# A two-layer transformer tower: in its first layer GpSimd divides the third weight and makes the state B's product with v and its count, and that weight's scales are made ahead of the mixes

## The chip, the cores and the metric

The kernel runs on one core of a Trainium2 chip (trn2). The metric is the time of one execution on the device in microseconds (us). It is the median of a few runs; one further execution was taken by the profiler, and all rows of a trace below come from that one. The engines are called PE (TensorE, matrix products), DVE (VectorE), ACT (ScalarE), POOL (GpSimd) and SP (the queue that issues most DMAs). Each runs its own list of instructions in order and waits on semaphores that others raise.

## What is computed

64 images are cut into 16 patches each and embedded in 256 features; with a class token that makes 64 x 17 = 1088 tokens. Layer 0 adds a recurrent attention and a feed-forward part whose weights and tokens are rounded to 4-bit values with a scale for each block of 16; layer 1 adds softmax attention with 16 heads and a mixture of 64 experts. The change is in the attention and in the preparation of the feed-forward weights of layer 0:

```python
# x: the normalised tokens; xx: the same, shifted by one token inside an image
# k, v, r = (x * mu_s + xx * (1 - mu_s)) @ W_s          (three "mixes")
def step(carry, inp):
    A, Bacc = carry
    kt, vt, ct, mt = inp          # ct = max(t - 1, 0), mt = (t > 0)
    out = A + jnp.exp(u + kt) * (vt * Bacc + ct)
    ek = jnp.exp(kt)
    A = e_dec * A + mt * ek * vt
    Bacc = e_grow * Bacc + mt / ek
    return ((A, Bacc), out)
# attention = (sigmoid(r) * out) @ Wo, added to h

def fake_quant_nvfp4(x, global_scale):       # of gate, up and down weights, and of tokens
    amax = max |x| of a block of 16
    sc8 = e4m3(clip(amax / 6 * global_scale, 0, 448)); dq = sc8 / global_scale
    a = clip(|x| / dq, 0, 6)                 # "divides"
    return sign(x) * nearest_fp4(a) * dq
```

global_scale of a weight is 448 * 6 / max|w| over the whole matrix.

## The kernel before, in words

Features lie on the 128 partitions in two halves (o or c = 0, 1), tokens along the free dimension (N = 1088, image by image, T = 17). Tokens by rows are kept in `h` in 9 tiles of 128 (NT). A layer norm is made in two parts, tiles 0 to 5 and 6 to 8 (LN_PARTS): ACT takes squares (L1172), DVE makes the variance `veps` (L1487, `ln_variance`), POOL raises it to -1/2 (L595, `ln` of POOL), DVE finishes it with one step of Newton (L1493 to L1497, `ln_finish`), ACT writes the normalised tile `xn` (L1180), PE transposes it (L726) and ACT moves it to `nT` (L1189).

Then, all in lists written out by hand:

- ACT makes six shifted copies of `nT`, one for each of k, v, r and half (L1234); DVE adds the unshifted part in six mixes (L1616), in the same order; PE multiplies them with the weights in six groups of 4 column quarters (L786, order k0, v0, k1, v1, r0, r1); ACT evacuates them: exp(k) to `ekk` and exp(-k) to `dB` (L1258, L1260), v to `vv` (L1265), sigmoid(r) to `sig` (L1256). `s_rkv_ev` counts the quarters, 4 a group.
- DVE's states, for each half o: the scan of B into `sB` (L1628), the input of A (L1632), B's product with v (L1637), the scan of A into `sA` (L1639), the count added to B's product (L1642), times exp(u) and exp(k) (L1643), the sum (L1646), and the gate with sigmoid(r) (L1623, `gated_state`), written over `vv`, which raises `s_y0`. A `link` waits for the end of an operation before the next.
- PE multiplies the gated halves with the output weight (L805, 8 tiles of half 0 after the first `s_y0`, 8 of half 1 after the second, then both of the last tile), and DVE adds them to `h` (L1468).

The third (down) weight is prepared among this: `weight_maxima(2)` on DVE (L1554, L1561), `largest(2)`, an all-reduce over partitions on POOL (L600), which stands in POOL's list behind both pows of the first norm; `weight_scales(2)` on DVE between the two first operations of the scans (L1565 to L1569, L1502 to L1512, then `weight_divide`, L1537, two operations of 128x1024); ACT's absolute value (L1198, `weight_size(2)`), behind the evacuation of r; DVE's rounding (L1516 and L1520) before and between the additions to `h`. The scales read the all-reduce's result, the division reads the scales.

POOL does the division for the nine tiles of hidden values later in the layer (L623), in the same form as the third weight's.

The last stage of layer 1 waits for nine semaphores `s_back`, one for each tile of rows brought back by DMA, from SP's list.

Of the kernel before, what the change touches and what calls it, by code (L numbers as in the profile page):

```python
# [15 lines left out]
ALU = mybir.AluOpType  # L16
# [9 lines left out]
CH = 4  # L26
# [82 lines left out]
def build(nc, A, out):  # L109
    with ExitStack() as ctx:  # L110
        def sem(name):
            return ctx.enter_context(nc.semaphore(name))

        def sems(name, n):
            return [sem(f"{name}{i}") for i in range(n)]
# [232 lines left out]
        s_scanz = sem("s_scanz")  # L348
        s_scanA = sem("s_scanA")
        s_wdiv = sem("s_wdiv")  # L350
# [86 lines left out]
        s_slot = sem("s_slot")  # L437
        s_back = sems("s_back", NT)
        s_sum = sem("s_sum")
# [127 lines left out]
        def _(pool):  # L567
# [29 lines left out]
            def largest(m):  # L597
# [12 lines left out]
                                    pattern=[[1, P]], channel_multiplier=-1).then_inc(s_mc, 1)  # L610
            ln(0, 0)
            ln(0, 1)
            largest(2)
            ln(1, 0)
# [99 lines left out]
        def _(pe):  # L714
# [426 lines left out]
            def row_sums(t):  # L1141

                pe.wait_ge(s_back[t], 16)
                for k in range(TOPK):
                    mm = nc.tensor.matmul(ps[0:rows(t), SUM_BANK[t], 0:D], ident[0:rows(t), 0:rows(t)],
                                          picked[t][0:rows(t), k * D:(k + 1) * D], start=False, stop=(k == TOPK - 1))
                mm.then_inc(s_sum, 1)
# [306 lines left out]
        def _(dve):  # L1454
# [22 lines left out]
            def after(count):  # L1477
                dve.wait_ge(s_dve, count)
# [52 lines left out]

            def weight_divide(x, scale, m):

                if m == 2:
                    for j in range(2):
                        v = x[:, j * I0:(j + 1) * I0].rearrange("p (k b r) -> p k b r", k=PAIRS, r=2)
                        ins = V.tensor_tensor(v, v, bc(bc(scale[:, j * NHB:(j + 1) * NHB], 1, PAIRS), 3, 2), ALU.mult)  # L1537
                    return ins
                x = x.rearrange("p (b k) -> p b k", k=BLK)
                return V.tensor_tensor(x, x, bc(scale, 2, BLK), ALU.mult)  # L1540
# [22 lines left out]
            def weight_scales(m):  # L1563
                dve.wait_ge(s_wmxa, m + 1)
                link(V.reciprocal(gsc[:, m:m + 1], wmx_all[:, m:m + 1]))  # L1565
                link(V.tensor_scalar(gsc[:, m:m + 1], gsc[:, m:m + 1], 448.0 * 6.0, None, ALU.mult))
                link(V.tensor_scalar(gs6[:, m:m + 1], gsc[:, m:m + 1], 1.0 / 6.0, None, ALU.mult))
                link(V.reciprocal(gin[:, m:m + 1], gsc[:, m:m + 1]))
                link(V.tensor_scalar(gil[:, m:m + 1], gin[:, m:m + 1], -(1.0 - 2.0 ** -23), None, ALU.mult))  # L1569
                link(block_scales(wam[:, m, :], [wsc[:, i, :] for i in range(3)], wscm, wscb[0] if m == 2 else wscb[m][:, 0:NBW], m, m == 2))  # L1570
                weight_divide(wraw[m], wsc[:, 2, :], m).then_inc(s_wdiv, 1)

# [37 lines left out]
            V.memset(dB.rearrange("p c (b t) -> p (c b) t", t=T)[:, :, 0:2], 0.0).then_inc(s_scanz, 1)  # L1610
            ln_finish(0, 1)
            dve.wait_ge(s_mixz, 4)
            for i, s in enumerate((1, 2, 0)):
# [10 lines left out]

            for o in range(DC):
                dve.wait_ge(s_d0, 7)
                dve.wait_ge(s_rkv_ev, (2 * o + 1) * CH)
                done_b = mark(V.tensor_tensor_scan(sB[o], d0[:, 2 * o + 1, :], dB[:, o, :], 0.0, ALU.mult, ALU.add))  # L1628
                if o == 0:
                    weight_scales(2)  # L1630
                dve.wait_ge(s_rkv_ev, (2 * o + 2) * CH)
                done_a = mark(V.tensor_tensor(dA[:, o, :, 2:T], by_t(ekk[:, o, :])[:, :, 1:T - 1],  # L1632
                                              by_t(vv[:, o, :])[:, :, 1:T - 1], ALU.mult))
                if o == 1:
                    gated_state(0)
                after(done_b)
                done_b = mark(V.tensor_tensor(sB[o], sB[o], vv[:, o, :], ALU.mult))  # L1637
                after(done_a)
                done_a = mark(V.tensor_tensor_scan(sA[o], d0[:, 2 * o, :], dA[:, o, :, :].rearrange("p b t -> p (b t)"), 0.0,  # L1639
                                                   ALU.mult, ALU.add))  # L1640
                after(done_b)
                link(V.tensor_tensor(by_t(sB[o]), by_t(sB[o]), bc(cnt, 1, B), ALU.add))  # L1642
                link(V.scalar_tensor_tensor(out=sB[o], in0=sB[o], scalar=eu[:, o:o + 1], in1=ekk[:, o, :],  # L1643
                                            op0=ALU.mult, op1=ALU.mult))
                after(done_a)
                link(V.tensor_tensor(sA[o], sA[o], sB[o], ALU.add))  # L1646
            gated_state(1)

# [310 lines left out]
            def add_rows_of(t):  # L1959

                r = slice(0, rows(t))
                dve.wait_ge(s_back[t], 16)
                p = picked[t][r, :].rearrange("p (k d) -> p k d", k=TOPK)
# [82 lines left out]
```

## Time and profile before

| | us |
|---|---|
| median of 3 runs | 623.29 |
| lowest and highest | 622.12, 624.65 |
| the profiled execution, its own time | 625.0 |
| its span in the trace | 623.3 |
| DVE busy | 439.4 (70%) |
| PE busy | 518.0 (83%) |
| ACT busy | 337.6 (54%) |
| POOL busy | 218.7 (35%) |

The profiled execution took 1.7 us more than both its span and the median. Start times below are in us from the start of the span. In a row of a timeline stand the start, the time in us, the engine, the line, the operation, the tile written and those read, shapes and count; in brackets, how long the engine had been idle before it and what ended that ("issue": nothing that the profile shows). `region` is the name of two large buffers from which most tiles are cut. Spans on POOL are rough.

### The profile page before, as it was taken

The page shows a single profiled execution, that of the slowest core. Times are in us where ns is not written, and L with a number is a line of the kernel's source. Part 1 is how long each engine was busy: PE and PEld are TensorE (multiplying, and loading weights), DVE is VectorE, ACT ScalarE, POOL GpSimd, SP SyncE. Part 2 cuts the span into 40 slices and gives each one's busy share as a digit, 9 for nine tenths or more (in the row PEclk, how much of TensorE's full clock was granted, in tenths as well). Part 3 has the DMA queues.
Part 4 walks back from the last instruction along what each step waited for, and adds up shares of the span by engine and source line. Part 5 has one row for each costly group of instructions (what it writes and reads, how often), then busy time and mean ns, then how long its engine had stood idle before and what let it go on. Part 6 is the DMA issues. An engine that isn't in the chain of part 4 may idle for free.

```text
span 623.3 us, 10367 instructions
## 1 busy us (share of the span) xinstructions
PE 518.0 (83%) x3494; PEld 421.2 (68%) x3498; DVE 439.4 (70%) x995; ACT 337.6 (54%) x798; POOL 218.7 (35%) x230
## 2 busy tenths in 40 slices
PE   3986953166555699999999999999999999999875
PEld 2755842023323699999999887876777777777674
DVE  4996998999999546555655713576776777775676
ACT  1577635255444656666666325625666677676600
POOL 2101001022422602222221141237777777777600
PEclk9985987586875699999999999999999999999979
DMA  8980000008200000000000001013777777887492
GB/s 270 381 315 0 1 0 0 0 2 272 79 2 0 1 26 27 26 28 27 26 1 2 2 1 51 22 28 100 200 225 203 230 237 216 230 241 212 143 407 87
DMA packets 43895, 67.33 MB, mean 108 GB/s; under 512 B 11022, under 2 KB 27015, under 8 KB 43716
## 3 DMA queue, kind: packets, MB, share of 16 engines
q1 hardware_dynamic: 36868, 64.62, 32.5%
q0 software_dynamic: 6976, 2.07, 1.7%
q8 instruction: 28, 0.46, 0.3%
q14 instruction: 23, 0.19, 0.1%
HBM read 66.81 MB, written 17.20 MB: 135 GB/s over the span
## 4 chain that ended last, share of the span: by engine, by line
PE 60%; DVE 24%; DMA 5%; ACT 4%; issue 3%; POOL 3%; SPq 0%; DVEq 0%; POOLq 0%; ACTq 0%
PE ps L1089 9%; PE ps L734 6%; PE ps L736 6%; PE ps L735 6%; PE ps L953 5%; PE ps L911 5%; PE ps L786 4%; PE ps L741 4%; DMA region<-x_rows,region 3%; PE ps L943 3%; PE ps L1079 2%; PE ps L925 2%; PE ps L1136 2%; DVE region L1724 2%; PE ps L1097 2%
## 5 line engine op out<-in xcount | busy, mean ns | idle before, releaser
L1089 PE MATMUL ps<-region 128*128 128x352 f32 x256 | 86.4, 460 | 0.3 <-issue 0.3
L1780 DVE TENSOR_TENSOR region<-ps,region 32x136 f32<-32x136 f32 x128 | 38.1, 298 | 55.3 <-PE ps L911 53.8
L685 POOL DMA_INDIRECT region<-x_rows,region x64 | 68.1, 1064 | 20.2 <-issue 15.0
L734 PE MATMUL ps<-nTh,high 128*128 128x272 f32 (+2 forms) x248 | 74.4, 300 | 0.4 <-ACT region L1362 0.4
L735 PE MATMUL ps<-nTl,high 128*128 128x272 f32 (+2 forms) x248 | 71.6, 289 | 0.0
L694 POOL DMA_INDIRECT y_rows<-region x60 | 61.1, 1019 | 21.0 <-issue 14.7
L644 POOL COPY region<-region 32x544 f32<-32x544 f32 x32 | 26.4, 825 | 115.1 <-DVE region L1799 113.6
L1928 DVE SCALAR_TENSOR_TENSOR region<-region,ps 128x176 f32<-128x176 f32 x64 | 25.4, 397 | 42.9 <-ACT region L1439 40.3
L736 PE MATMUL ps<-nTh,pairs_low 128*128 128x272 f32 x192 | 55.6, 290 | 0.0
L1449 ACT ACTIVATE high<-region 88x512 fp32r<-88x512 f32 x64 | 40.3, 630 | 25.4 <-PE ps L736 20.0
L1089 PEld LDWEIGHTS ps<-region 128*128 128x128 f32 x256 | 43.6, 190 | 14.0 <-issue 0.5
L734 PEld LDWEIGHTS ps<-nTh,high 128*128 128x128 f32 (+2 forms) x248 | 46.3, 187 | 2.0 <-ACT region L1362 0.6
L735 PEld LDWEIGHTS ps<-nTl,high 128*128 128x128 f32 (+2 forms) x248 | 46.4, 187 | 0.1
L595 POOL TENSOR_TENSOR rstd<-veps,mhalf 128x6 f32<-128x6 f32 (+1 forms) x8 | 9.2, 1148 | 100.6 <-DVE veps L1487 100.6
L734 PE MATMUL ps<-high,pairs_low 88*128 88x256 f32 x128 | 41.3, 323 | 3.0 <-DVE shared_low L1953 3.0
L623 POOL TENSOR_TENSOR region<-region 128x1024 f32<-128x1024 f32 x9 | 19.2, 2129 | 63.3 <-DVE region L1754 63.3
L741 PE MATMUL ps<-region 128*128 128x256 f32 (+1 forms) x108 | 28.6, 420 | 10.2 <-DMA region<-patches 10.2
L736 PEld LDWEIGHTS ps<-nTh,pairs_low 128*128 128x128 f32 x192 | 36.5, 190 | 0.0
L735 PE MATMUL ps<-w_low,pairs_low 88*128 88x256 f32 x128 | 36.1, 282 | 0.0
L736 PE MATMUL ps<-high,pairs_low 88*128 88x256 f32 x128 | 36.0, 281 | 0.0
L911 PE MATMUL ps<-region 128*128 128x136 f32 x256 | 33.1, 282 | 0.9 <-DVE region L1780 0.9
L953 PE MATMUL ps<-region 128*128 128x256 f32 (+1 forms) x144 | 31.8, 381 | 2.0 <-DVE region L1780 1.5
(264 smaller groups left out, 1353.4 us busy)
## 6 DMA issues: line engine op xcount, KB each, us to landing
region<-moe_w SPq DMA_DIRECT2D x64, 352.0 KB, 3.7
region<-moe_w SPq DMA_DIRECT2D x64, 176.0 KB
y_rows<-zrow SPq DMA_DIRECT2D x1, 6528.0 KB, 25.3
region<-y_rows SPq DMA_DIRECT2D x8, 768.0 KB, 10.5
region<-wqkv SPq DMA_DIRECT2D x8, 384.0 KB, 3.0
region<-ffn_w SPq DMA_DIRECT2D x2, 1024.0 KB, 8.3
region<-patches SPq DMA_DIRECT2D x3, 384.0 KB, 8.3
region<-patches SPq DMA_DIRECT2D x1, 1152.0 KB, 10.7
```

The costliest lines, as they stand in the source:

```text
L644: nc.gpsimd.tensor_copy(pbd[j][r, :, q * T:(q + 1) * T], prT[r, :, 0:T]).then_inc(s_spread, 1)
L685: nc.gpsimd.indirect_dma_start(out=xb[m8], out_offset=None, in_=x_rows, in_offset=bass.IndirectOffsetOnAxis(ap=sloti[:, at:at + 1], axis=0 ...
L694: nc.gpsimd.indirect_dma_start(out=y_rows, out_offset=bass.IndirectOffsetOnAxis(ap=sld[m8], axis=0), in_=yb[m], in_offset=None, bounds_che ...
L734: nc.tensor.matmul(out, parts_a[0], parts_b[0], start=first, stop=False)
L735: nc.tensor.matmul(out, parts_a[0], parts_b[1], start=False, stop=False)
L736: return nc.tensor.matmul(out, parts_a[1], parts_b[0], start=False, stop=last)
L741: nc.tensor.matmul(ps[0:rows(t), t % 8, 0:D], patch[:, c, t * P:t * P + rows(t)], tokw[:, c, :], start=(c == 0), stop=False)
L911: mm = nc.tensor.matmul(ps[:, 4 + g // 2, (g % 2) * 2 * GW:(g % 2 + 1) * 2 * GW], qT[:, 4 * t:4 * t + 4, :].rearrange("p b t -> p (b t)"), ...
L953: mm = nc.tensor.matmul(ps[0:rows(t), 4 + t % 4, 0:D], attnT[:, c, t * P:t * P + rows(t)], wo1[:, c, :], start=(c == 0), stop=(c == HP - 1))
L1089: mm = nc.tensor.matmul(ps[:, 2 + m % 2, 0:2 * EI], xbT[m % 2][:, c, :], w13[m][:, c, :], start=(c == 0), stop=(c == DC - 1))
L1449: nc.scalar.activation(w2_h[m % 2], w2[m], ACT.Copy).then_inc(s_w2h, 1)
L1780: last = V.tensor_tensor(sc[r, s0:s0 + 8, 0:T].rearrange("p (a b) t -> p a b t", a=4), ps[r, 4:8, 0:4 * GW].rearrange("p a (b h t) -> p a ...
```

## The change

The first layer's lists are changed on POOL and DVE:

- POOL: `largest(2)` moves from behind the second pow to between the two pows. Behind the second pow POOL now waits for the third weight's scales (`s_wrec`) and divides that weight in two operations, and then, for each half, waits for the scan of B (`s_scanB`) and for v (`s_rkv_ev`), multiplies `sB` with `vv` and adds the count (`s_scanP`).
- DVE: `weight_scales(2)` moves from behind the first scan to behind `ln_finish(0, 1)`, ahead of the mixes, and no longer divides. The product with v and the count are gone from DVE's list. The order of the states is new: scan B0, input A0, scan A0, scan B1, sum of half 0, input A1, scan A1, gate 0, sum of half 1, gate 1.
- The nine semaphores of the last stage are no longer their own: eight are those of the first loads, and the number waited for is raised by what they already hold.

```diff
-        s_back = sems("s_back", NT)
+        s_back = [*s_first, *s_patch, *s_qw, sem("s_back8")]
+        BACK = [32] * 3 + [16] * 5 + [0]
...
             ln(0, 0)
+            largest(2)
             ln(0, 1)
-            largest(2)
+            pool.wait_ge(s_wrec, 1)
+            for j in range(2):
+                v = wraw[2][:, j * I0:(j + 1) * I0].rearrange("p (k b r) -> p k b r", k=PAIRS, r=2)
+                ins = nc.gpsimd.tensor_tensor(v, v, bc(bc(wsc[:, 2, j * NHB:(j + 1) * NHB], 1, PAIRS), 3, 2), ALU.mult)
+            ins.then_inc(s_wdiv, 1)
+            for o in range(DC):
+                by_image = sB[o].rearrange("p (b t) -> p b t", t=T)
+                pool.wait_ge(s_scanB, o + 1)
+                pool.wait_ge(s_rkv_ev, (2 * o + 2) * CH)
+                nc.gpsimd.tensor_tensor(sB[o], sB[o], vv[:, o, :], ALU.mult).then_inc(s_scanP, 1)
+                pool.wait_ge(s_scanP, 2 * o + 1)
+                nc.gpsimd.tensor_tensor(by_image, by_image, bc(cnt, 1, B), ALU.add).then_inc(s_scanP, 1)
             ln(1, 0)
...
-                link(block_scales(wam[:, m, :], ...))
-                weight_divide(wraw[m], wsc[:, 2, :], m).then_inc(s_wdiv, 1)
+                last = block_scales(wam[:, m, :], ...)
+                if m == 2:
+                    last.then_inc(s_wrec, 1)
+                else:
+                    link(last)
+                    weight_divide(wraw[m], wsc[:, 2, :]).then_inc(s_wdiv, 1)
...
             ln_finish(0, 1)
+            weight_scales(2)
             dve.wait_ge(s_mixz, 4)
...
+            def state_sum(o, done_a):
+                dve.wait_ge(s_scanP, 2 * o + 2)
+                link(V.scalar_tensor_tensor(out=sB[o], in0=sB[o], scalar=eu[:, o:o + 1], in1=ekk[:, o, :],
+                                            op0=ALU.mult, op1=ALU.mult))
+                after(done_a)
+                link(V.tensor_tensor(sA[o], sA[o], sB[o], ALU.add))
+
+            dve.wait_ge(s_d0, 7)
+            done_a = [0, 0]
+            for o in range(DC):
+                dve.wait_ge(s_rkv_ev, (2 * o + 1) * CH)
+                V.tensor_tensor_scan(sB[o], d0[:, 2 * o + 1, :], dB[:, o, :], 0.0, ALU.mult, ALU.add).then_inc(s_scanB, 1)
+                if o == 1:
+                    state_sum(0, done_a[0])
+                dve.wait_ge(s_rkv_ev, (2 * o + 2) * CH)
+                link(V.tensor_tensor(dA[:, o, :, 2:T], by_t(ekk[:, o, :])[:, :, 1:T - 1],
+                                     by_t(vv[:, o, :])[:, :, 1:T - 1], ALU.mult))
+                done_a[o] = mark(V.tensor_tensor_scan(sA[o], d0[:, 2 * o, :], dA[:, o, :, :]..., 0.0, ALU.mult, ALU.add))
+            gated_state(0)
+            state_sum(1, done_a[1])
             gated_state(1)
...
-                dve.wait_ge(s_back[t], 16)
+                dve.wait_ge(s_back[t], BACK[t] + 16)
```

## Rows read from the trace of the kernel before

**Rows 1.** The chain of waits, 40 to 102 us: start, us, what.

```profile
55.43 23.87 PE ps L786 x92
...
93.20 2.21 DVE region L1516
```

**Rows 2.** Timeline of DVE, 30 to 75 us.

```profile
38.35 0.29 DVE L1561 TENSOR_REDUCE wmx<-region 128x1 f32<-128x128 f32 x1
...
45.01 2.29 DVE L1548 TENSOR_TENSOR region<-region 128x2048 bf16<-128x2048 bf16 x1
...
48.64 0.10 DVE L1493 TENSOR_TENSOR nwt<-rstd 128x3 f32<-128x3 f32 x1
...
53.94 7.66 DVE L1616 SCALAR_TENSOR_TENSOR region<-nT,region 128x1088 f32<-128x1088 f32 x6 [4.39 <-ACT region L1234]
62.89 2.42 DVE L1628 TENSOR_TENSOR_SCAN region<-region 128x1088 f32<-128x1088 f32 x1 [1.29 <-ACT region L1260]
65.23 0.14 DVE L1565 RECIPROCAL gsc<-wmx_all 128x1 f32<-128x1 f32 x1
...
68.85 2.36 DVE L1537 TENSOR_TENSOR region<-region 128x1024 f32<-128x1024 f32 x2
71.13 1.15 DVE L1632 TENSOR_TENSOR region<-region 128x960 f32<-128x960 f32 x1
```

**Rows 3.** Timeline of POOL, 0 to 180 us.

```profile
13.77 0.38 POOL L600 PARTITION_ALL_REDUCE wmx_all<-wmx  x1 [9.55 <-issue]
...
36.16 1.38 POOL L595 TENSOR_TENSOR rstd<-veps,mhalf 128x6 f32<-128x6 f32 x1 [18.48 <-DVE veps L1487]
47.46 0.86 POOL L595 TENSOR_TENSOR rstd<-veps,mhalf 128x3 f32<-128x3 f32 x1 [9.93 <-DVE veps L1487]
54.20 1.33 POOL L600 PARTITION_ALL_REDUCE wmx_all<-wmx  x1 [5.88 <-issue]
101.28 1.74 POOL L595 TENSOR_TENSOR rstd<-veps,mhalf 128x6 f32<-128x6 f32 x1 [45.76 <-DVE veps L1487]
```

**Rows 4.** Lines 600 and 595: durations in ns, then first and last start.

```profile
L600 POOLq MODIFY_POOL_CONFIG  x4: 11/14/18, 4.1 to 48.6; - x4
...
L595 POOLq MODIFY_POOL_CONFIG  x4: 7/44/83, 17.7 to 55.5; - x4
```

**Rows 5.** The page: DMA busy in 40 slices of 15.6 us, in tenths.

```profile
DMA  8980000008200000000000001013777777887492
```

**Rows 6.** Timeline of POOL, 180 to 226 us.

```profile
188.39 2.12 POOL L623 TENSOR_TENSOR region<-region 128x1024 f32<-128x1024 f32 x1 [5.18 <-DVE region L1754]
...
213.09 5.16 POOL L636 TENSOR_TENSOR h<-h,region 128x2304 f32<-128x2304 f32 x1 [4.45 <-DVE nTl L1767]
```

**Rows 7.** Timeline of DVE, 183 to 192 us.

```profile
183.55 1.21 DVE L1724 SCALAR_TENSOR_TENSOR region<-region 128x1024 f32<-128x1024 bf16 x1
...
188.54 3.06 DVE L1724 SCALAR_TENSOR_TENSOR region<-region 128x1024 f32<-128x1024 bf16 x1
```

**Rows 8.** Timeline of all engines, 203.5 to 209 us.

```profile
204.08 4.58 DVE L1495 TENSOR_SCALAR nwt<-nwt 128x3 f32<-128x3 f32 x1
...
204.88 3.77 POOL L632 MEMSET region<- 128x2176 f32 x2
```

**Rows 9.** Timeline of ACT, 40 to 165 us.

```profile
65.58 0.40 ACT L1265 ACTIVATE region<-ps 128x272 f32<-128x272 f32 x1 [0.52 <-PE ps L786]
```

**Rows 10.** Groups of DVE by form: busy us, mean ns, idle before.

```profile
L1637 DVE TENSOR_TENSOR region<-region 128x1088 f32<-128x1088 f32 x2 | 2.6, 1284 | 0.0
...
L1642 DVE TENSOR_TENSOR region<-region 128x1088 f32<-128x1088 f32 x2 | 2.5, 1267 | 0.0
```

**Rows 11.** Timeline of PE, 79 to 100 us.

```profile
80.04 1.06 PE L774 MATMUL ps<-ident_bf,region 128*128 128x128 bf16 x16
84.49 5.38 PE L805 MATMUL ps<-region 128*128 128x256 f32 x16 [3.39 <-DVE region L1623]
93.25 6.42 PE L805 MATMUL ps<-region 128*128 128x256 f32 x20 [3.39 <-DVE region L1623]
```

More of the change, by code:

```diff
@@ L348, in build @@
         s_scanz = sem("s_scanz")
-        s_scanA = sem("s_scanA")
+        s_scanB = sem("s_scanB")
+        s_scanP = sem("s_scanP")
+        s_wrec = sem("s_wrec")
         s_wdiv = sem("s_wdiv")
@@ L1141, in row_sums @@
             def row_sums(t):
-                pe.wait_ge(s_back[t], 16)
+                pe.wait_ge(s_back[t], BACK[t] + 16)
                 for k in range(TOPK):
@@ L1530, in round_fp4, with weight_divide @@
                 link(clamp(q))
[L1532 to L1538, printed above, removed]
+            def weight_divide(x, scale):
                 x = x.rearrange("p (b k) -> p b k", k=BLK)
@@ L1569, in weight_scales @@
                 link(V.tensor_scalar(gil[:, m:m + 1], gin[:, m:m + 1], -(1.0 - 2.0 ** -23), None, ALU.mult))
-                link(block_scales(wam[:, m, :], [wsc[:, i, :] for i in range(3)], wscm, wscb[0] if m == 2 else wscb[m][:, 0:NBW], m, m == 2))
-                weight_divide(wraw[m], wsc[:, 2, :], m).then_inc(s_wdiv, 1)
+                last = block_scales(wam[:, m, :], [wsc[:, i, :] for i in range(3)], wscm, wscb[0] if m == 2 else wscb[m][:, 0:NBW], m, m == 2)
+                if m == 2:
[3 more added lines that the diff above has]
+                    weight_divide(wraw[m], wsc[:, 2, :]).then_inc(s_wdiv, 1)
             def round_weight(m):
@@ L1623, in gated_state @@
                 V.tensor_tensor(vv[:, o, :], sA[o], sig[:, o, :], ALU.mult).then_inc(s_y0, 1)
[L1625 to L1642, printed above, removed]
+            def state_sum(o, done_a):
+                dve.wait_ge(s_scanP, 2 * o + 2)
                 link(V.scalar_tensor_tensor(out=sB[o], in0=sB[o], scalar=eu[:, o:o + 1], in1=ekk[:, o, :],
@@ L1646, in _ @@
                 link(V.tensor_tensor(sA[o], sA[o], sB[o], ALU.add))
+            dve.wait_ge(s_d0, 7)
[8 more added lines that the diff above has]
+                                     by_t(vv[:, o, :])[:, :, 1:T - 1], ALU.mult))
+                done_a[o] = mark(V.tensor_tensor_scan(sA[o], d0[:, 2 * o, :], dA[:, o, :, :].rearrange("p b t -> p (b t)"), 0.0,
+                                                      ALU.mult, ALU.add))
+            gated_state(0)
+            state_sum(1, done_a[1])
             gated_state(1)
```

## The prediction

> **What bounds the kernel now.** The page's busy shares cover two layers and say nothing about the first alone, so I begin with the chain of waits around the edit [rows 1]: 92 matmul pieces of the mixes carry it from 55.43 for 23.87, and then VectorE (DVE) alone carries it to 93.20, when the last gated product is done, and beyond. Next the same stretch by engine. DVE's timeline [rows 2] shows three things: 4.39 us of idle time before the mixes at 53.94 (it waits for ACT's shifted copy), the third weight's scales and division from 65.23 to 71.13, and unbroken work from 71.13 to 93.20. GpSimd's (POOL's) timeline [rows 3] is nearly empty: a pow at 36.16, a pow at 47.46, an all-reduce at 54.20 after 5.88 of idle time that no producer explains, and nothing more until 101. So DVE is the bound from 79.3 on, and POOL looks free. Two things about POOL are to be priced: what an all-reduce costs beside a pow, and whether POOL and DVE can work side by side.
>
> **The change, part by part.**
>
> **(a) Scales moved ahead of the mixes.** They take 68.85 - 65.23 = 3.6 us, and their cover is the 4.39 of idle time from 49.55 [rows 2]. Ended at 53.2, they leave 0.7 before the first mix at 53.94. Cost nothing, gain 3.6 on DVE. If their input came late, this cover would be gone; see (b).
>
> **(b) The third all-reduce moved between the two pows.** Its input is ready at 38.64 (38.35 + 0.29) [rows 2], so no data are missing. But POOL's queue runs a pair of configuration instructions whenever it goes from other arithmetic to the all-reduce, and again from the all-reduce to the pow: one set from 4.1 to 48.6 for the all-reduce's line, one from 17.7 to 55.5 for the pow's [rows 4]. After the pair at 48.6 the all-reduce starts at 54.20, 5.6 later; after the pair at 4.1 it starts at 13.77, 9.6 later, and both waits have the releaser "issue", not an input [rows 3, 4]. The first fell in a slice in which the DMA engines were 80 to 90% busy, the second in one where they did nothing [rows 5]. What the way back to the pow costs is not seen: before, 18.5 and 45.8 us of waiting for veps covered it. In the new order both switches and the all-reduce lie between the first pow's end, 37.54, and the second pow's start, 47.46: 9.9 us. The first switch, half of it beside full DMA, takes 5.6 to 9.6, I say 8, to 45.8. The all-reduce then meets DVE's multiplication of 45.01 to 47.3, and its own record of 1.33 beside a DVE operation (0.38 at 13.77) says it waits for that: done at 47.5. Bounds for the way back are 0 below (a gain is excluded, since it stood in nobody's way) and 9.6 above; I take 5.6, the row with idle DMA engines, as they will be. The pow then runs from 53.1 to 54.0 (0.86) instead of ending at 48.32, and the first operation behind it on DVE starts at 54.1, not 48.64 [rows 2]: **+5.5 us**. Behind it in a row stand DVE's finish of the norm, ACT's norm of the last tiles, their transposes, the shifted copies and all mixes, with nothing else for any of these engines to do: all of it is on the chain. With a first switch of 5.6 (all-reduce done by 44.3) it would be 2.5; with a way back of 9.6, 9.5.
>
> The Trainium skill (GPSIMD Engine Reference, § 2.1 Instruction dispatch) says that the first call to a freshly loaded kernel pays an IRAM load of about 6 us, 5.95 as measured there, with no profile instruction to be seen. The 5.6 agrees with it, and no run here shows whether the pow's return is such a call. By that figure for the return, the term would be 5.8.
>
> **(c) Division, product and count on POOL, beside DVE.** The divide's form is in the trace: 128x1024, 2.12, and so twice 2.1. For the 1088-wide product and count the nearest plain row is 2304 wide in 5.16 [rows 6], 2.24 ns an element: 2.4 each, four of them 9.8. That would be hidden, were they side by side. The rows say that they are not: at 188.54 a DVE operation with two operands in SBUF started beside a divide of 188.39 to 190.51 and took 3.06, where the same one at 183.55 took 1.21 [rows 6, 7]. It ended 1.1 after the divide, so it ran from 0.1 before the divide's end. All DVE operations from the mixes to the last gated product read two operands from SBUF. I therefore put POOL's and DVE's pieces end to end, with 0.12 saved at each handover.
>
> First the divide: it can begin at 53.2, just ahead of the first mix at 53.94, and its two halves follow each other with no wait between. When POOL's memsets followed each other so, a DVE operation on three elements a partition stood for 4.58, to the end of the last one [rows 8]. So I let both halves pass: 53.2 + 4.2 = 57.4, first mix (7.66 / 6 = 1.3) done at 57.4 - 0.1 + 1.3 = 58.6 instead of 55.3. Matmuls start +3.2 later, and being back to back they hand the 3.2 on to ACT's evacuation of v: from 65.98 (65.58 + 0.40) [rows 9] to 69.2. Then, DVE: 93.20 - 71.13 = 22.1 less the two products and two counts that leave, 2.6 + 2.5 [rows 10], is 17.0; POOL's four, 9.8; eight handovers, -1.0. Sum: 69.2 + 17.0 + 9.8 - 1.0 = 95.0; with 0.2 for semaphores between them 95.2, against 93.20: **+2.0 us**. This includes what (a) gained. If the mix gets in between the halves, matmuls slip by only 1.2 and the sum is 0.0.
>
> **(d) What follows.** The first half of the output products needs 5.38, the second 6.42, and they begin 8.8 apart, each at its gated product [rows 11]. In the new order only three operations of about 1.3 lie between these, 3.9, so the first half ends 1.5 after the second gate; DVE's rounding of 2.2 [rows 1], which stands before the first addition, covers that. Cost 0, up to 0.6 if the second half is no quicker for following the first at once. Weight abs on ACT and the semaphores shared by the last stage: 0; the latter only change the number waited for. Nothing later is tied to the clock of the first layer; the shift is carried to the end.
>
> Sum: 5.5 + 2.0 = 7.5 on a span of 623.3. The profiled execution took 625.0, 1.7 above the median of 623.29, so I add the 7.5 to the median: **630.8 us**.
>
> **The rivals.**
> *The way back to the pow costs nothing* (for: at 36.16 and 101 the pow starts at once; against: the waits there would hide 5.6, and the same pair costs 5.6 the other way). Then only (c) counts, 0.0 to +2.0: 623.3 to 625.3, no change.
> *DVE and POOL run side by side in these forms, and the way back is free: faster.* Place: the stretch behind v's evacuation. v is there at 65.98, DVE's remaining 17.0 plus 0.7 of waiting for POOL and ACT end at 83.7, 9.5 earlier; then TensorE, free of its transposes at 81.1 (80.04 + 1.06), is the bound: 81.1 + 5.4 + 6.4 = 92.9 instead of 99.7 (93.25 + 6.42) [rows 11]: -6.8, 616.5 us. It decides if the lock costs under 2 us in all. Against it stands the 3.06 [rows 7]. With the switch charged, the same mechanism gives -6.8 + 5.5: 622.0, within 0.5%.
> *The edit leaves the work where it was*: no; the all-reduce has no other place to go, and scales and division wait for it.
>
> **How the numbers follow.** The likeliest, both terms: 0.70, its own range 626 (2.5 and 0) to 634.8 (9.5 and 2.0). Switch back free, lock holds: 0.18. Side by side and free: 0.04; side by side, switch charged: 0.05. Other: 0.03. A measurement of this kernel can tell about 0.5%, 3.1 us, from no change. Of the first case 0.64 lies above 626.4 and 0.06 below; with 0.01 of the second and 0.01 of the others slower is 0.66. Same is 0.06 + 0.17 + 0.03 (the fourth) = 0.26. Faster is the third's 0.04 and 0.02 each of the fourth and of others, 0.08. The range takes in the first two cases whole, from 622.5 to 634.8.
>
> **What would show it.** Right: the second pow starts near 53 after an idle stretch put down to issue, the first mix's record is over 3 us long, DVE has records of 3 to 5 us in the scans' stretch, and the last gated product ends near 100.7. Wrong: a pow at 47.5; scans of 2.42 and gates of 1.29 beside POOL's products; or a gap before the mixes of the old 4.4 us less 3.6.

## The result, and the profile after

| | before | after |
|---|---|---|
| median of the runs, us | 623.29 | 628.72 |
| lowest to highest (5 runs each) | 622.12 to 624.65 | 627.53 to 629.49 |
| the profiled execution, us | 625.0 | 629.49 |
| its span, us | 623.3 | 627.6 |

The changed kernel is slower: ratio 1.008, interval 1.0061 to 1.01; the medians differ by 5.4 us. The forecast was 630.8, slower, within 622.5 to 634.8. Sign and mechanisms stand, but the sum of 7.5 does not: the first layer gives 3.5, and the other 1.9 of the medians' difference arise behind it, from a cause that stays open. Line numbers have moved: POOL's pow is L598 and its all-reduce L603 in the kernel after, most other lines are 10 to 15 higher, and the states are at L1652 (scan of B), L1656 (input of A), L1658 (scan of A), L1643 (times exp(u) and exp(k)), L1646 (sum) and L1638 (gate).

First GpSimd, where both mechanisms meet. The timeline of POOL in the kernel after, 30 to 110 us (start, us, engine, line, operation, count, in brackets the idle time before it and what ended it):

```profile
35.37 1.38 POOL L598 TENSOR_TENSOR rstd<-veps,mhalf 128x6 f32<-128x6 f32 x1 [17.74 <-DVE veps L1502]
42.81 0.69 POOL L603 PARTITION_ALL_REDUCE wmx_all<-wmx  x1 [6.06 <-issue]
50.65 0.90 POOL L598 TENSOR_TENSOR rstd<-veps,mhalf 128x3 f32<-128x3 f32 x1 [7.15 <-issue]
56.14 5.00 POOL L620 TENSOR_TENSOR region<-region 128x1024 f32<-128x1024 f32 x2 [4.59 <-DVE region L1527]
70.32 3.40 POOL L626 TENSOR_TENSOR region<-region 128x1088 f32<-128x1088 f32 x1 [9.18 <-ACT region L1280]
73.79 4.33 POOL L628 TENSOR_TENSOR region<-region 128x1088 f32<-128x1088 f32 x1
80.48 3.51 POOL L626 TENSOR_TENSOR region<-region 128x1088 f32<-128x1088 f32 x1 [2.36 <-DVE region L1652]
84.07 3.25 POOL L628 TENSOR_TENSOR region<-region 128x1088 f32<-128x1088 f32 x1
```

And the configuration instructions of the kernel after, by line (durations in ns, then first and last start):

```profile
L598 POOLq MODIFY_POOL_CONFIG  x4: 6/44/83, 17.7 to 43.5; - x4
L603 POOLq MODIFY_POOL_CONFIG  x4: 11/14/18, 4.1 to 37.0; - x4
```

The all-reduce, which stood at 54.20 after the second pow [rows 3], is at 42.81, and the pow has gone from 47.46 to 50.65. Both stand behind an idle stretch put down to "issue". The pairs are where the prediction put them: the one at 37.0 costs until 42.81, the one at 43.5 until 50.65. Against rows 3, POOL's other pieces in this stretch are new.

The same stretch on DVE, kernel after, 36 to 110 us:

```profile
51.58 0.16 DVE L1508 TENSOR_TENSOR nwt<-rstd 128x3 f32<-128x3 f32 x1 [3.58 <-POOL rstd L598]
...
56.94 10.40 DVE L1631 SCALAR_TENSOR_TENSOR region<-nT,region 128x1088 f32<-128x1088 f32 x6 [0.88 <-ACT region L1249]
67.26 2.42 DVE L1652 TENSOR_TENSOR_SCAN region<-region 128x1088 f32<-128x1088 f32 x1
70.20 1.16 DVE L1656 TENSOR_TENSOR region<-region 128x960 f32<-128x960 f32 x1 [0.53 <-ACT region L1280]
71.40 4.60 DVE L1658 TENSOR_TENSOR_SCAN region<-region 128x1088 f32<-128x1088 f32 x1
75.92 4.48 DVE L1652 TENSOR_TENSOR_SCAN region<-region 128x1088 f32<-128x1088 f32 x1
80.32 1.32 DVE L1643 SCALAR_TENSOR_TENSOR region<-region 128x1088 f32<-128x1088 f32 x1
81.68 3.46 DVE L1646 TENSOR_TENSOR region<-region 128x1088 f32<-128x1088 f32 x1
85.17 3.16 DVE L1656 TENSOR_TENSOR region<-region 128x960 f32<-128x960 f32 x1
...
94.60 1.29 DVE L1638 TENSOR_TENSOR region<-region 128x1088 f32<-128x1088 f32 x1
```

Against rows 2: the 4.39 us before the mixes have shrunk to 0.88, since the scales fill them, and scales and division are gone from between the scans. In exchange the mixes take 10.40 in place of 7.66, a scan 4.60 and 4.48 in place of 2.42, an addition 3.46 in place of 1.3. Lay the two timelines over each other: each long DVE record lies beside a long POOL record, and each ends some 1.1 us (addition, input A) or 2.3 us (scan) after POOL's has. The last gated product ends at 95.9 where it ended at 93.2.

One marker carries the comparison from here on: ACT's first squares of the next norm, which need everything in this stretch. The timeline of ACT in the kernel before, then in the kernel after, 90 to 100 us:

```profile
95.90 0.51 ACT L1172 ACTIVATE xn<-h,mom 128x256 f32<-128x256 f32 x1 [11.63 <-DVE h L1468]
```

```profile
98.60 0.51 ACT L1187 ACTIVATE xn<-h,mom 128x256 f32<-128x256 f32 x1 [10.14 <-DVE h L1483]
```

### The profile page after: what moved, and what is told of

The parts are those of the page before. It is cut to its first block, busy times and chain, and to the rows that moved or that the text cites. A ratio compares the mean times of both kernels' runs of the same rounds, so it can differ in the third digit from the quotient of the medians.

```text
span 627.6 us, 10369 instructions
## 1 busy us (share of the span) xinstructions
PE 517.9 (83%) x3494; PEld 421.1 (67%) x3498; DVE 443.4 (71%) x989; ACT 337.3 (54%) x798; POOL 237.0 (38%) x236
## 4 chain that ended last, share of the span: by engine, by line
PE 56%; DVE 26%; DMA 6%; issue 5%; ACT 3%; POOL 3%; SPq 1%; POOLq 0%; DVEq 0%; ACTq 0%
PE ps L1104 8%; PE ps L749 6%; PE ps L751 6%; PE ps L750 6%; PE ps L968 5%; PE ps L926 5%; DMA region<-x_rows,region 4%; PE ps L756 3%; PE ps L958 3%; PE ps L1094 2%; PE ps L940 2%; PE ps L1151 2%; DVE region L1739 2%; PE ps L801 2%; PE ps L1112 1%
## 5 line engine op out<-in xcount | busy, mean ns | idle before, releaser
L598 POOL TENSOR_TENSOR rstd<-veps,mhalf 128x6 f32<-128x6 f32 (+1 forms) x8 | 9.2, 1149 | 68.1 <-DVE veps L1502 60.9
```

## The experiments

Each edit is against the kernel before unless its diff says otherwise. The chips differ: the kernel before takes 658 us on the two that ran e1 to e8, and 623 on the one that ran e9 to e12, with the same first layer; so ratios are compared, and times within the first 215 us. All were timed beside the kernel before on their own chip.

The executions also differ in when the first patches arrive. S below is ACT's first eviction of a patch product. P is the start of the second pow, Q that of the first squares of the next norm. In the old order P - S is the same in every profile, 27.68 to 27.70, so P - S prices the all-reduce's place, and Q - P what the scales' place, the division, product and count do. Q - P still scatters by up to 0.7 where DVE's list behind P is the same: 48.44 in the kernel before and 47.72 in e1. The granted clock of the 12.5 us from the first mix on differs between these two, 0.73 and 0.79 (0.75 in both e3 and e4), but it does not order all of them: the kernel after has 47.95 at 0.68 and e10 48.24 at 0.76. Differences in Q - P under 0.7 are therefore read as no more than a sign.

| | S | P | P - S | Q | Q - P |
|---|---|---|---|---|---|
| before | 19.77 | 47.46 | 27.69 | 95.90 | 48.44 |
| e9 (before, semaphores shared) | 19.27 | 46.97 | 27.70 | 95.31 | 48.34 |
| after | 18.99 | 50.65 | 31.66 | 98.60 | 47.95 |
| e10 (after, own semaphores) | 19.07 | 50.50 | 31.43 | 98.74 | 48.24 |
| e1 (all-reduce between the pows) | 19.09 | 51.07 | 31.98 | 98.79 | 47.72 |
| e2 (after, all-reduce early) | 19.01 | 47.58 | 28.57 | 95.61 | 48.03 |
| e3 (before, all-reduce early) | 19.78 | 47.68 | 27.90 | 96.09 | 48.41 |
| e4 (e3 and scales ahead) | 19.59 | 47.52 | 27.93 | 92.30 | 44.78 |
| e8 (the kernel of e4 again) | 19.21 | 47.49 | 28.28 | 91.91 | 44.42 |
| e5 (e4, division on POOL) | 19.09 | 47.63 | 28.54 | 91.56 | 43.93 |

### e1: the all-reduce between the pows, and nothing else

```diff
             ln(0, 0)
+            largest(2)
             ln(0, 1)
-            largest(2)
```

> The kernel before with one edit: the third all-reduce stands between the two pows of the first norm. Scales, division, product and count stay on DVE, where they were. Theory 1 (the way to the all-reduce and the way back to the pow each cost POOL about 6 to 7 us, with no instruction of the profile in that time): the second pow starts about 7 us after the all-reduce's end, near 51 instead of 47.5, and the kernel takes 3.5 to 5 us more than before, about 627.5. Theory 2 (the loss of the change comes from POOL and DVE in each other's way, the switch being free): the second pow starts at 47.5 and the time is that of before, 623.3.

Ratio 1.0053 (1.0018 to 1.0089). POOL's timeline in e1, 34 to 60 us:

```profile
35.48 1.38 POOL L595 TENSOR_TENSOR rstd<-veps,mhalf 128x6 f32<-128x6 f32 x1 [17.79 <-DVE veps L1487]
43.57 0.76 POOL L600 PARTITION_ALL_REDUCE wmx_all<-wmx  x1 [6.72 <-issue]
51.07 0.90 POOL L595 TENSOR_TENSOR rstd<-veps,mhalf 128x3 f32<-128x3 f32 x1 [6.73 <-issue]
```

This one move gives both idle stretches, and P - S is 4.3 longer than in the kernel before. The rival by which the way back costs nothing has fallen. Both ways cost the same here, 6.72 and 6.73.

### e3 and e2: the all-reduce ahead of both pows, in the kernel before and after

```diff
+            largest(2)
             ln(0, 0)
...
             weight_scales(1)
+            weight_maxima(2)
             round_weight(0)
             ln_variance(0, 0)
-            weight_maxima(2)
-            ln_finish(0, 0)
             dve.wait_ge(s_wabs, 2)
             link(round_up(wraw[1], wqb[1]))
+            ln_finish(0, 0)
```

`largest(2)` leaves its old place. e3 is this in the kernel before, e2 in the kernel after.

> The kernel before with only the earlier maxima and the earlier all-reduce of the run above, the scales where they were. It is the control of the other two: both theories expect the time of before, 623.3, within 1 us; more than that would be the price of the new order on DVE or of a late first pow, and has to be taken off from the others.

> The changed kernel with the third all-reduce done before the first pow: DVE takes the third weight's block maxima ahead of the rounding of the first weight, and POOL makes the all-reduce right behind the first two and the masks, so that it goes to the pow only once, in a stretch in which it waits anyway. All else as changed. Theory 1: the second pow starts at its old time, near 47, and the kernel takes about 4 us less than the changed one, near 624.7. Theory 2 (switch free): no gain, 628.7. If the one way back to the pow lasts beyond 36 beside the full DMA queues, the first pow is late and part of the 4 us stays.

e3: ratio 0.9999 (0.9974 to 1.0025). e2: 1.0032 (1.0 to 1.0063), with Q - S 3.0 shorter than in the kernel after. POOL's timeline in e2, 4 to 60 us:

```profile
29.89 2.31 POOL L603 PARTITION_ALL_REDUCE wmx_all<-wmx  x1 [12.20 <-DVE wmx L1571]
39.25 1.63 POOL L598 TENSOR_TENSOR rstd<-veps,mhalf 128x6 f32<-128x6 f32 x1 [7.05 <-issue]
47.58 0.86 POOL L598 TENSOR_TENSOR rstd<-veps,mhalf 128x3 f32<-128x3 f32 x1 [6.70 <-DVE veps L1502]
```

Only the switch back to the pow is left in this stretch, and it again costs 7.05 of idle time: the first pow starts at 39.25 where it stood at 36.16. But nothing that ends the stretch waits for the first pow, so the second is held by its input again, and e3 is as fast as the kernel before. The early order is thus a place for the all-reduce that costs nothing. The memset and the mask operations behind an all-reduce need no such switch: in e2 a memset starts at 16.06, right behind the all-reduce of 15.84 to 16.19. In e2 the second pow follows its S by 28.57, 0.9 more than in the old order, its input being the later (6.70 us of waiting for it); that part is of the experiment and not of the change. Q - P is free of it: 48.03, against 48.41 in e3. So scales ahead, division, product and count together gain 0.4 here, and 0.3 by the two pairs before and e9 against after and e10 (48.39 and 48.10): about nothing, within the scatter of Q - P.

### e4 and e8: scales ahead of the mixes, everything else on DVE

```diff
             ln_finish(0, 1)
+            weight_scales(2, False)
             dve.wait_ge(s_mixz, 4)
...
-                    weight_scales(2)
+                    weight_divide(wraw[2], wsc[:, 2, :], 2).then_inc(s_wdiv, 1)
```

on top of e3; `weight_scales(m, False)` leaves the division out.

> The kernel before with the early all-reduce and with the third weight's scales ahead of the mixes, its division, product and count left on DVE. Theory 1: the scales' 3.6 us fall into DVE's idle time of 4.4 before the mixes, and nothing is late: 3 to 3.6 us faster than before, near 620, faster than both kernels. Theory 2 says the same of this one. Rival: the time ahead of the mixes isn't free (the mixes start later), and the gain is under 1 us.

> The kernel of e4 again, beside the others, so that e5 can be read against it on one chip: 3 to 3.6 us faster than before.

Ratios 0.9953 (0.9922 to 0.9984) and 0.9945 (0.9918 to 0.9971): faster than the kernel before. Q - P falls by 48.41 - 44.78 = 3.63 against e3 at the same granted clock, the 3.6 of step (a); e8 gives 4.0 at a clock of 0.78.

### e5: the division on POOL, product and count on DVE

```diff
+            pool.wait_ge(s_wrec, 1)
+            for j in range(2):
+                ...
+                ins = nc.gpsimd.tensor_tensor(v, v, bc(...), ALU.mult)
+            ins.then_inc(s_wdiv, 1)
```

on top of e4, with DVE's division left out.

> The kernel of e4 with the third weight's division alone given to POOL, right behind its scales, as in the change; product and count stay on DVE. Theory A (POOL's and DVE's operations exclude each other while both read SBUF): the two halves, some 2.1 each alone, stand in the way of the first and second mix; two mixes have records of 2.3 to 3.1 instead of 1.34, DVE's end moves by 4.2 less the 0.8 before the first mix less the 2.3 that leave DVE: about +1 against e4. Theory B (they run side by side): mixes of 1.34, and 2.3 us faster than e4.

Ratio 0.9953 (0.9931 to 0.9975), e4's own. DVE's timeline in e5, 44 to 92 us:

```profile
54.10 10.46 DVE L1623 SCALAR_TENSOR_TENSOR region<-nT,region 128x1088 f32<-128x1088 f32 x6 [0.88 <-ACT region L1239]
64.48 2.41 DVE L1635 TENSOR_TENSOR_SCAN region<-region 128x1088 f32<-128x1088 f32 x1
```

The mixes pay 2.8 for the division (2.7 in the kernel after), and then no 2.34 of division and no wait of 0.89 stands between the mixes and the scan (below, the timeline of DVE in e8, 44 to 92 us):

```profile
62.55 2.43 DVE L1630 TENSOR_TENSOR_SCAN region<-region 128x1088 f32<-128x1088 f32 x1 [0.89 <-ACT region L1260]
64.89 2.34 DVE L1537 TENSOR_TENSOR region<-region 128x1024 f32<-128x1024 f32 x2
```

So Q - P is 0.5 to 0.9 shorter than in e8 and e4, where I had expected it some 1 us longer: a miss in sign, too small for the times. The division is neutral on POOL. The product and the count are not: e2 has all of e5 and these two besides, with the new order of the states, and its Q - P is 48.03 - 43.93 = 4.1 longer. No run separates the new order from the product and count.

### e6 and e7: POOL's work added to the kernel before

```diff
             largest(2)
+            pool.wait_ge(s_rkv_ev, 8)
+            for _ in range(4):
+                nc.gpsimd.tensor_tensor(xn[..., 0:N], xn[..., 0:N], xn[..., N:2 * N], ALU.mult).then_inc(s_dummy, 1)
+                pool.wait_ge(s_dummy, _ + 1)
```

(The tile's `rearrange` is left out of these lines.) e6 adds four linked products of 128x1088 on a tile that nobody uses then; e7 in their place five linked memsets of 128x2176, which read nothing. ACT's squares wait for the last.

> The kernel before with work added: POOL makes four linked products of 128x1088 f32, both operands and result in a tile that nobody needs at that time, from v's first evacuation on, beside the scans. DVE's list is untouched. Theory A: each product takes DVE's place for 2.0 to 2.3 us; DVE's scans and products beside them have records longer by that, and the kernel takes 8 to 9 us more than before. Theory B: no more than 0.5 us.

> The kernel before with POOL writing the same tile with five linked memsets of 128x2176 f32 (1.9 us each, 9.5 in all) in the same place: it writes SBUF and reads nothing. If it is POOL's reading that excludes a two-operand operation of DVE, scans, products and sums keep their 2.42, 1.28 and 1.29, and only the small one-operand operations of the scales wait, once for at most two memsets: 0 to +3 us, all of it in the scales. If any use of SBUF by POOL excluded DVE's, it would be 8 to 9 us more, as in e6.

e6: ratio 1.0127 (1.0092 to 1.0161), Q - P 56.88, +8.5. POOL's timeline in e6, 30 to 92 us:

```profile
64.58 10.19 POOL L616 TENSOR_TENSOR xn<-xn 128x1088 f32<-128x1088 f32 x4 [9.89 <-ACT region L1269]
```

and DVE's, 44 to 92 us:

```profile
67.19 2.53 DVE L1508 TENSOR_SCALAR region<-region 128x128 bf16<-128x128 f32 x1
69.76 2.59 DVE L1509 SCALAR_TENSOR_TENSOR region<-region 128x128 f32<-128x128 bf16 x1
```

The size is what serial work gives (10.19 less handovers), but the place is another than I had meant: the products met the scales, not the scans. Small operations of DVE each stand for a whole product: L1509 takes 2.59 here and 0.29 in e7 below. One-operand operations wait too: L1508 takes 2.53, and 0.23 where POOL is idle (e11). POOL's rate is plain as well: four products in 10.19, 2.55 each with the handover.

e7: ratio 1.0087 (1.0057 to 1.0118), Q - P 52.60, +4.2, more than I had expected. The profiled execution (656.55) is the fastest of e7's seven, whose median is 664.39, so the trace may not show all that the memsets cost in the others. POOL's timeline in e7, 44 to 100 us:

```profile
65.96 9.79 POOL L616 MEMSET xn<- 128x2176 f32 x5 [10.48 <-ACT region L1269]
```

and DVE's, 44 to 92 us:

```profile
67.98 1.93 DVE L1508 TENSOR_SCALAR region<-region 128x128 bf16<-128x128 f32 x1
69.95 0.29 DVE L1509 SCALAR_TENSOR_TENSOR region<-region 128x128 f32<-128x128 bf16 x1
70.28 0.43 DVE L1511 SCALAR_TENSOR_TENSOR region<-region 128x256 bf16<-128x256 bf16 x1
70.74 1.15 DVE L1516 TENSOR_SCALAR region<-region,gil 128x128 f32<-128x128 bf16 x1
...
72.91 2.36 DVE L1542 TENSOR_TENSOR region<-region 128x1024 f32<-128x1024 f32 x2
```

Beside memsets the one-operand `TENSOR_SCALAR` operations wait (1.93 and 1.15, where e11's same operations, with POOL idle, take 0.23 and 0.29), while the two-operand ones in the same stretch do not, the small ones (0.29 and 0.43) as little as the division, 2.36 as in the kernel before. The scans say nothing, as they come behind the last memset, which ends at 75.75. The waits of L1507 (1.86 for 0.29), L1508 and L1516 add up to 4.1, the whole of the +4.2. Not every one-operand operation waits, though: the reciprocal behind them stands beside memsets too and takes 0.95, as in the kernel before. So POOL's products hold back DVE's `TENSOR_SCALAR` operations and the two-operand ones, its memsets only the `TENSOR_SCALAR` ones. The Trainium skill (SBUF — State Buffer, § Who interferes with whom) says that a DVE instruction with two SBUF inputs contends with a GpSimd instruction that reads SBUF and not with one that only writes it; both runs agree, 2.59 against 0.29 for the same operation. It also matters for the forecast: rows 8, of memsets and a one-operand operation, was not the row for a division beside a mix.

### e11: POOL's products beside the scans of e4

```diff
+            pool.wait_ge(s_scanA, 1)
+            for _ in range(4):
+                ...
+                pool.wait_ge(s_dummy, _ + 1)
```

e6's loop on top of e4. A semaphore that DVE raises behind the division, just ahead of the first input A, releases it, so that it meets the scans.

> The kernel of e4 (scales ahead of the mixes, all on DVE) with four linked products of 128x1088 f32 added on POOL, as in e6, but begun behind the third weight's division, so that they stand beside DVE's two-operand scans and products and not beside its small operations. POOL's part alone takes 2.49 (e6). If they exclude each other, DVE's operations beside them are longer by 2.1 to 2.3 each, four times, and the first layer ends 8 to 9 us later than e4's; in the change the same four, in place of 5.1 on DVE, then cost 3 to 4 us net. If only small operations suffer: under 2 us.

Ratio 1.0107 (1.0065 to 1.0148); Q - P 53.77 (Q at 101.26, P at 47.49), 9.0 longer than in e4, for four products of 2.55 in e6. POOL's timeline in e11, 44 to 92 us:

```profile
67.67 14.87 POOL L617 TENSOR_TENSOR xn<-xn 128x1088 f32<-128x1088 f32 x4 [19.33 <-DVEq L1641]
```

and DVE's:

```profile
68.56 3.59 DVE L1647 TENSOR_TENSOR region<-region 128x1088 f32<-128x1088 f32 x1
72.07 4.70 DVE L1649 TENSOR_TENSOR_SCAN region<-region 128x1088 f32<-128x1088 f32 x1
76.70 3.50 DVE L1652 TENSOR_TENSOR region<-region 128x1088 f32<-128x1088 f32 x1
80.23 3.46 DVE L1653 SCALAR_TENSOR_TENSOR region<-region 128x1088 f32<-128x1088 f32 x1
```

Four DVE operations are each 2.1 to 2.3 longer than alone (1.28, 2.42, 1.27 and 1.35), near the 2.5 of one product, and POOL's four take 14.87 in place of 10.19: they take turns. The products compute nothing that is used, and only ACT's squares wait for the last, which ends at 82.5, 19 us before they start; so the turns alone do this.

### e9 and e10: the shared semaphores of the last stage

```diff
-        s_back = sems("s_back", NT)
+        s_back = [*s_first, *s_patch, *s_qw, sem("s_back8")]
+        BACK = [32] * 3 + [16] * 5 + [0]
...
-                dve.wait_ge(s_back[t], 16)
+                dve.wait_ge(s_back[t], BACK[t] + 16)
```

e9 is this in the kernel before (TensorE's wait changes alike); e10 undoes it in the kernel after.

> The kernel before with one edit, the last stage's nine semaphores shared as in the change. Open: the changed kernel's median is 5.4 above before, while its first layer ends only 2.7 to 3.5 later in the profiles, and e2 shows the same surplus. If the shared semaphores cost something in the last stage, this one is 1 to 2 us slower than before; if the surplus is scatter of the expert stage, it is before's time within the interval.

> The changed kernel with nine semaphores of their own for the last stage. If the shared ones cost 1 to 2 us, it is that much faster than 628.7 against 623.3 (ratio 1.005 or less); if not, the ratio is the changed kernel's 1.008.

e9: ratio 0.999 (0.9963 to 1.0016). In the kernel before the shared semaphores cost nothing that shows, at most 1.0 us. e10: 1.0064 (1.0036 to 1.0091), +3.3 us, where the change without e10's edit has +5.4; the two intervals overlap. The kernel after was not timed beside e10, so a cost of sharing in that kernel alone is not excluded. e10's twelve times fall into two groups, 621.96 to 624.22 (five) and 626.33 to 628.81 (seven). So do the 26 of the kernel before on this chip: 618.47 to 620.61 (six) and 622.31 to 625.85 (twenty). Group against group, by the groups' medians, e10 is 3.6 and 3.8 slower (623.63 against 619.99, 627.13 against 623.37), little more than the first layer's 3.5.

The place that makes two groups is most likely the third norm, at 200 to 212 us, which the change does not touch. DVE's timeline in the kernel after, 195 to 213 us:

```profile
206.89 4.58 DVE L1510 TENSOR_SCALAR nwt<-nwt 128x3 f32<-128x3 f32 x1
```

POOL's in the kernel after, 180 to 213 us:

```profile
206.41 0.90 POOL L644 MEMSET region<- 128x960 f32 x1
207.25 0.50 POOL L645 MEMSET region<- 128x480 f32 x1
207.69 3.77 POOL L647 MEMSET region<- 128x2176 f32 x2
```

DVE's in e10, 195 to 213 us:

```profile
206.94 0.87 DVE L1509 TENSOR_SCALAR nwt<-nwt 128x3 f32<-128x3 f32 x1
```

The same one-operand operation on three elements begins within 0.1 us of the same moment beside the same four memsets, and either gets in behind the second of them (0.87) or stands until the last has ended (4.58), as it did in rows 8. Of the fourteen profiles five show the long form (before, after, e1, e8, e11), eight the short, and e12 below neither. From that operation's start to the first eviction of the attention's projections it is 9.43 or 9.44 us in every long case and 5.35 to 5.37 in five of the eight short ones; in the other three (e2, e5, e6) it is 6.65 or 6.66, and in e2's trace TensorE's transposes and projections there are the slower ones (matmuls of 0.43 us where e3 has 0.29). So one execution differs from the next by 2.8 or 4.1 us with no edit at all; e4 and e8, the same kernel, have one form each. The profiled executions of e9 and e10 (620.39 and 621.96) have the short form and lie in the lower groups, that of the kernel before (625.0) has the long form and lies in the upper; that the form decides the group in the other executions is inferred.

### e12: the memsets behind the norm

```diff
             pool.wait_ge(s_down, NT)
+            pool.wait_ge(ln_scale, 6)
             nc.gpsimd.memset(vT[:, :, T:SLOT], 0.0).then_inc(s_zero, 1)
```

on top of e4.

> The kernel of e4 with one wait more on POOL: the memsets ahead of the second layer's attention wait until DVE has finished the third norm. In the trace of before a tensor_scalar on three elements stood 4.58 us behind them, and ACT and TensorE waited for that norm. If that is on the chain, this one is 2 to 4.4 us faster than e4; if the memsets are then late for the attention, part of it comes back.

617.91 us (615.39 to 619.14), ratio 0.9926 (0.9897 to 0.9954) with the kernel before at 623.22 on the same chip. DVE's timeline in e12, 195 to 213 us:

```profile
200.12 0.17 DVE L1496 TENSOR_SCALAR nwt<-nwt 128x3 f32<-128x3 f32 x1
```

and POOL's, 180 to 213 us:

```profile
200.81 0.90 POOL L630 MEMSET region<- 128x960 f32 x1 [1.12 <-DVE shift L1498]
```

The operation takes its 0.17, and the first eviction comes 5.37 us behind its start, as in the better short cases. This is the fastest kernel of the study, 5.3 us under the kernel before and 8.6 under e10 on the same chip. Against e4 and e8 (0.9953, 0.9945) the gain is 0.2 to 0.3%, 1.2 to 1.7 us, less than the 2 to 4.4 expected and within the intervals; what is shown of the wait alone is the record.

## Why the prediction was right or wrong

**(a) Scales ahead: right.** Predicted gain 3.6; 3.63 between e3 and e4. Their cover was there: 0.88 us of idle time stays before the mixes, where 0.7 was forecast.

**(b) The all-reduce between the pows: right in kind, mis-sized.** Predicted +5.5, measured +4.0 (P - S longer by 4.0 in the kernel after, 3.7 in e10, 4.3 in e1), within the bounds of 2.5 and 9.5. From the first pow's end to the second's end I put 16.4 us; it was 51.55 - 36.75 = 14.8. Three terms moved:
- The first switch: 8 from its pair taken "half of it beside full DMA", 5.8 measured (37.0 to 42.81; 6.06 of idle time from the pow's end). 2.2 too much. The reason for the surcharge has fallen with it: the DMA engines moved 387 GB/s from 37.0 to 42.8 in the kernel after, a full load all through this switch and not for half of it, and it still cost about what it costs beside idle ones (5.6 in the kernel before). So DMA traffic is not what made the 9.6 at the start of the kernel; what did stays open.
- As the all-reduce came at 42.81 and not at 45.8, the multiplication at 45 no longer stood in its way: 0.69 in place of 1.7. 1.0 too much, and it hung on the first error.
- The way back: 5.6 taken from the other direction, 7.15 measured. 1.5 too little. The Trainium skill (GPSIMD Engine Reference, § 2.1 Instruction dispatch) gives about 6 us for a first call to a freshly loaded kernel. The way there agrees: behind a pow it is 5.86 to 6.11 of idle time in six profiles and 6.72 in e1. The way back to a pow takes more, 6.73 to 7.29 in the ten profiles in which no wait covers it (the least in e1, the most in e4).

**(c) POOL and DVE end to end: right in kind, and the wrong one of its two cases.** DVE records of 3 to 4.6 us stand in the scans' stretch, and product and count, with the new order of the states, cost 4.1 in e2 against e5, for which the forecast's terms give 9.8 - 1.0 - 5.1 = 3.7. What failed is "So I let both halves pass": from the idle stretch before the mixes I sent both halves of the division ahead of the first mix. They take turns with the mixes. The single records of the kernel after show it; on DVE, 56.5 to 59.1 us and then 59.3 to 62.2:

```profile
56.94 2.35 DVE L1631 SCALAR_TENSOR_TENSOR region<-nT,region 128x1088 f32<-128x1088 f32 x1 [0.88 <-ACT region L1249]
...
59.21 3.08 DVE L1631 SCALAR_TENSOR_TENSOR region<-nT,region 128x1088 f32<-128x1088 f32 x1
```

and on POOL, in the same stretch:

```profile
56.14 2.00 POOL L620 TENSOR_TENSOR region<-region 128x1024 f32<-128x1024 f32 x1 [4.59 <-DVE region L1527]
...
58.10 3.04 POOL L620 TENSOR_TENSOR region<-region 128x1024 f32<-128x1024 f32 x1
```

The first half ends at 58.14, the first mix follows and ends at 59.29, the second half at 61.14, the second mix at 62.29. The first mix was done 1.0 later than alone, not 3.2, and the weights' matmuls began by so much earlier. The prediction named this case and gave it 0.0; taken with (a), Q - P came out at -0.3. I had chosen between the two by rows 8, whose operations are of another kind (e7), and whose long form is one of two that occur (e10 has the other). The -0.3 can't be told from the 0.0 of the named case, as Q - P scatters by up to 0.7; from +2.0 it can.

**(d) What follows: right.** 2.71 us from the last gated product's end to the first squares, 2.70 before. The output products of both halves run in one piece; TensorE's timeline in the kernel after, 79 to 110 us:

```profile
92.03 9.97 PE L820 MATMUL ps<-region 128*128 128x256 f32 x36 [6.74 <-DVE region L1638]
```

9.97 for what took 5.38 and 6.42 apart [rows 11], and DVE's rounding covered it as expected.

**The signs that were named.** The second pow starts at 50.65 behind an idle stretch of issue, not near 53; the first mix's record is 2.35, not over 3; the last gated product ends at 95.9, not near 100.7. In both times 0.8 of the miss comes from this execution's patches, which arrived earlier. The records of 3 to 5 us in the scans' stretch are there. One sign of being wrong was badly drawn: a gap before the mixes of 4.4 less 3.6 is what step (a) itself forecast, as 0.7, and it came as 0.88.

**The sum.** 4.0 - 0.3 = 3.7 in place of 7.5; Q, set against its own S, is 3.5 later in the kernel after and in e10 than in the kernel before. The medians' 5.4 holds 1.9 more. The two-valued stretch at 200 us does not explain it: both profiled executions have the long form, and the five runs of the kernel before, 622.12 to 624.65, lie at the upper group that this kernel shows on the chip of e9 to e12 (lowest there 622.31, the other group ends at 620.61). Of the kernel after's five, 627.53 to 629.49, three lie in e10's upper group and two, 629.03 and 629.49, above it. Between the two profiles themselves, 2.8 us are there at the first eviction of the attention (213.51 and 216.32) and 1.5 more by the end of the span. The part behind that eviction scatters from 407.9 (e10) to 411.3 (after) in the profiles on chips of this speed, with 409.8 in the kernel before. Whether the 1.9 is such scatter over five runs, or a cost of the shared semaphores in the changed kernel alone, stays open; the interval's lower end, 1.0061, is 3.8 us.

So the forecast of 630.8 came 2.1 from the median partly by luck: 4.0 too much in the first layer, and 1.9 of slowdown from elsewhere that it had no term for. Nor did it reckon with a stretch that differs by some 4 us between executions, though rows 8 had shown its long form. The rival of a free way back is out by e1, the one of work side by side by e6 and e11.

## What to carry to other kernels

Look at POOL's order of operations as well as at its idle time: between an all-reduce and a pow it stands for 6 to 7 us each way here, so put the all-reduce where POOL waits anyhow (e3 cost nothing, the same move between two pows 4 us). When DVE is the bound and its operations read two operands from SBUF, a POOL operation that reads SBUF adds nearly its whole time (four products of 10.2 in all added 8.5 in e6 and 9.0 in e11); moving work of 1.3 us on DVE to 2.5 us on POOL is a loss, however empty POOL looks. Hold POOL's memsets until a chain of small one-operand DVE operations is through: in e12 that took a wait of 0.7 or 4.4 us off one of them, though the gain in time was within the intervals.

## What the runs showed of the hardware that I had not expected

- The way back from an all-reduce to a pow costs POOL as much as the way there or more: 7.15 and 6.06 us of idle time in the kernel after, 6.73 and 6.72 in e1. A memset behind an all-reduce pays nothing (16.06 in e2).
- Unlinked halves of a POOL division take turns with DVE operations queued back to back (2.35 and 3.08 for mixes of 1.34), while a one-operand operation beside four unlinked memsets is let in after two of them or after all four, 0.87 or 4.58 us, with the same kernel and the same moment of start.
- Memsets of POOL held `TENSOR_SCALAR` operations (1.93 for 0.23) and left a reciprocal (0.95) and two-operand operations beside them alone (0.29, and 2.36 for the division), while products of POOL held `TENSOR_SCALAR` and two-operand ones (2.53 and 2.59).
